# Infini-attention block on one NeuronCore: value products in three f16 parts

## The chip, the cores and the metric

The kernel runs on one NeuronCore of a Trainium2 chip. The metric is the device time of one execution in microseconds (us). Engines are named as in the profile: PE is TensorE (matmuls and its transposes), DVE VectorE, ACT ScalarE, POOL GpSimd, SP SyncE, which here only issues DMAs. Each engine works through its own list of instructions in order and waits at semaphores for the others.

## The reference

One block of two halves over x of shape (8, 512, 256) in f32: normalised attention with a compressive memory, then a coupled feed-forward part of three cycles. The change is in the attention. Its core, for segments of 128 rows and 16 heads of width 64:

```python
def step(carry, seg):
    M, Z = carry
    ...
    scores = jnp.einsum('bhid,bhjd->bhij', q, k) * scale
    scores = jnp.where(mask, -jnp.inf, scores)
    att_dot = jnp.einsum('bhij,bhjv->bhiv', jax.nn.softmax(scores, axis=-1), v)
    sq = jax.nn.elu(q) + 1.0
    att_mem = jax.lax.stop_gradient(sq @ M / (sq @ jnp.swapaxes(Z, -2, -1)))
    sk = jax.nn.elu(k) + 1.0
    M_new = M + jnp.einsum('bhld,bhlv->bhdv', sk, v)
    Z_new = Z + sk.sum(axis=-2, keepdims=True)
    att = gate * att_mem + (1.0 - gate) * att_dot
    out = att.reshape(B, LSEG, H * DV) @ Wo
    return ((M_new, Z_new), out)
```

The product that changes is the one of the softmax numerators with v (att_dot). A column of ones beside v gives the row sums, so that the division comes after the product: 65 columns for each head.

## The kernel before

**Staging.** Eight batches are taken as four pairs (bp), each with four segments (s): 16 steps, m = 4 bp + s. In a step the 32 units (2 batches by 16 heads) go in four groups (g) of 8 units, and a group's read-out in two halves of 4 units. Every engine has a hand-written function `step(bp, s)` that lists its work in order; nothing is scheduled by a program. After the 16 steps comes the feed-forward part (from about 880 us), which the change leaves alone.

**One group, in the order of its dependences.** PE computes scores (`scores`, L1266 to L1278, three f16 products of high and low parts of q and k) into the two banks `s_bank`. DVE takes the negated row maxima (`maxima`, L941). ACT exponentiates into Pr (`probs`, L658, 8 instructions). PE turns Pr, four units at a time, back into `s_bank` (`turn_probs`, L1288), and ACT copies the turned probabilities to the tile PT in f32 (`take_p`, L665, two instructions), which releases `s_bank` and the read-out (semaphore p_done). PE's `read_out` multiplies PT with V (L1301), sq with the memory M (L1307) and, after the second half, sk with V for the update of M (L1315). DVE divides by the row sums and adds the update (`divide`, L948 to L959). POOL mixes the memory and the dot part (`gated`, L467 to L471, three instructions for each half), and when all eight halves of a step are in, DVE transposes the result (`to_rows`, L1007) for the output projection (L1328, L1343).

**Beside it** PE computes the q, k and v of the next step (`project`, L1237, six pieces i = 0 to 5, 12 f16 matmuls of 512 columns each); DVE moves each piece out by a transpose (`take_x`, L916; pieces 4 and 5 are V) and so frees the banks `x_bank` for the next piece. `turn` (L1253) turns q and k of a group; ACT and DVE split them in high and low parts (`take_q`, L925 and L926; `take_k`, L934), and `scores` waits for both. ACT and POOL form elu(k) + 1 (`exp_k`, L647 and L651; `elu_k`, L452 and L454), not where s is 3.

**Orders that the prediction uses.** On PE a step is: scores(0), read_out(3,1) of the step before, project(0), turn_probs and turn of group 1, project(1), read_out(0,0), scores(1), turn_att, read_out(0,1), project(2), turn_att, turn_probs, project_out, turn, read_out(1,0), turn, project(3), scores(2), read_out(1,1), turn_probs and turn of group 3, project(4), read_out(2,0), scores(3), read_out(2,1), turn_probs and turn of the next group 0, read_out(3,0), project(5). In front of scores(1) DVE does take_x(5), maxima(0), divide(3,1), take_x(0), to_rows, take_q(1), take_k(1). to_rows waits until POOL has done gated(3,0) and gated(3,1) of the step before; POOL does them between elu_k(0) and elu_k(1). In front of scores(3) DVE ends with x2_norm (L876), take_q(3), take_k(3); at the end of a step it does take_x(4), take_q(0), take_k(0), divide(3,0), take_x(5), of which project(5) waits for take_x(4).

## Time and profile before

| | us |
|---|---|
| median of 3 runs | 1073.15 |
| lowest, highest | 1071.67, 1073.36 |
| the profiled execution | 1072.58 |
| its span, first to last instruction | 1070.8 |
| PE busy (matmul records) | 992.2, 93% |
| PEld busy (weight loads) | 698.9, 65% |
| DVE busy | 777.6, 73% |
| ACT busy | 635.1, 59% |
| POOL busy | 575.9, 54% |
| all L1301 matmul records (the f32 value products) | 136.0, 1024 records |

A matmul record lasts from its start to a modelled end, so records overlap; what one costs in a row of them is the distance between starts. An f32 matmul leaves two records, an f16 one leaves one. In brackets a timeline row has the idle time in front of it and what released it. The granted clock is 0.5 at 1.2 GHz and 1.0 at 2.4 GHz.

### The profile page before, as it was taken

The page shows a single profiled execution, that of the slowest core. Times are in us where ns is not written, and L with a number is a line of the kernel's source. Part 1 is how long each engine was busy: PE and PEld are TensorE (multiplying, and loading weights), DVE is VectorE, ACT ScalarE, POOL GpSimd, SP SyncE. Part 2 cuts the span into 40 slices and gives each one's busy share as a digit, 9 for nine tenths or more (in the row PEclk, how much of TensorE's full clock was granted, in tenths as well). Part 3 has the DMA queues.
Part 4 walks back from the last instruction along what each step waited for, and adds up shares of the span by engine and source line. Part 5 has one row for each costly group of instructions (what it writes and reads, how often), then busy time and mean ns, then how long its engine had stood idle before and what let it go on. Part 6 is the DMA issues. An engine that isn't in the chain of part 4 may idle for free.

```text
span 1070.8 us, 20177 instructions
## 1 busy us (share of the span) xinstructions
PE 992.2 (93%) x7748; PEld 698.9 (65%) x7748; DVE 777.6 (73%) x1399; ACT 635.1 (59%) x1364; POOL 575.9 (54%) x686
## 2 busy tenths in 40 slices
PE   5999999999999999999999999999999889999971
PEld 2677777776777777777777777777777765343431
DVE  6868687867777777768686868586959463588665
ACT  4756565556656564657474646474746454687863
POOL 4456565445656563456565635475747261456563
PEclk9999999999999999999999999999999989999995
DMA  7100000000000000000000000000000000300015
GB/s 187 32 21 1 21 2 21 2 21 1 21 2 21 2 21 1 21 1 21 1 21 2 21 2 21 1 21 1 12 2 16 18 11 10 157 1 1 1 40 118
DMA packets 16910, 23.92 MB, mean 22 GB/s; under 512 B 7344, under 2 KB 9136, under 8 KB 16304
## 3 DMA queue, kind: packets, MB, share of 16 engines
q1 hardware_dynamic: 15344, 18.58, 6.3%
q10 hardware_dynamic: 1472, 4.06, 1.1%
q8 instruction: 62, 1.02, 0.4%
q14 instruction: 32, 0.26, 0.1%
HBM read 13.97 MB, written 8.65 MB: 21 GB/s over the span
## 4 chain that ended last, share of the span: by engine, by line
PE 70%; DVE 19%; ACT 4%; POOL 3%; issue 3%; POOLq 0%; DVEq 0%; ACTq 0%
PE ps L1237 18%; PE ps L1343 11%; PE ps L1301 6%; PE ps L1278 5%; DVE arena L916 4%; PE ps L1470 4%; PE ps L1307 3%; PE ps L1483 3%; PE ps L1288 3%; PE ps L1328 3%; PE ps L1465 3%; PE ps L1253 3%; DVE arena L876 2%; PE ps L1315 2%; DVE arena L941 2%
## 5 line engine op out<-in xcount | busy, mean ns | idle before, releaser
L1237 PE MATMUL ps<-arena 128*128 128x512 f16 x1152 | 266.0, 381 | 5.2 <-DVE arena L893 3.1
L658 ACT ACTIVATE arena<-ps,arena 128x128 f32<-128x128 f32 x512 | 139.4, 387 | 96.1 <-DVE arena L941 96.1
L1237 PEld LDWEIGHTS ps<-arena 128*128 128x128 f16 x1152 | 110.2, 98 | 125.6 <-DVE arena L916 4.5
L916 DVE STREAM_TRANSPOSE arena<-ps 128x1024 f32<-128x1024 f32 x96 | 145.6, 1516 | 23.7 <-PE ps L1237 21.6
L467 POOL TENSOR_TENSOR arena<-arena 128x256 f32<-128x256 f32 x128 | 93.1, 728 | 125.0 <-DVE arena L951 82.0
L1301 PE MATMUL ps<-arena 128*128 128x65 f32 x1024 | 136.0, 276 | 5.9 <-ACT arena L665 4.8
L1301 PEld LDWEIGHTS ps<-arena 128*128 128x128 f32 x1024 | 127.5, 192 | 18.8 <-ACT arena L665 8.3
L868 DVE BATCH_NORM_STATS2 arena<-arena 128x6 f32<-128x256 f32 x100 | 36.9, 409 | 121.8 <-ACT arena L684 121.0
L1343 PE MATMUL ps<-arena 128*128 128x256 f32 x544 | 121.9, 382 | 0.3 <-ACT arena L672 0.3
L452 POOL TENSOR_TENSOR arena<-arena 128x512 f32<-128x512 f32 x48 | 73.2, 1526 | 86.9 <-ACT arena L651 86.6
L1343 PEld LDWEIGHTS ps<-arena 128*128 128x128 f32 x544 | 102.0, 190 | 16.1 <-ACT arena L672 1.4
L471 POOL TENSOR_TENSOR arena<-arena 128x256 f32<-128x256 f32 x128 | 95.2, 744 | 10.0
L420 POOL TENSOR_TENSOR arena<-arena 128x2 f32<-128x2 f32 x50 | 9.8, 195 | 167.6 <-DVE arena L872 167.6
L469 POOL TENSOR_TENSOR arena<-arena 128x256 f32<-128x256 f32 x128 | 93.4, 730 | 10.0
L665 ACT ACTIVATE arena<-ps 128x512 f32<-128x512 f32 x128 | 76.7, 615 | 33.6 <-PE ps L1288 33.6
L951 DVE TENSOR_TENSOR arena<-ps,arena 128x512 f32<-128x512 f32 x128 | 88.5, 691 | 4.4
L941 DVE TENSOR_REDUCE arena<-ps 128x4 f32<-128x512 f32 x128 | 80.8, 671 | 12.6 <-PE ps L1278 12.6
L1307 PE MATMUL ps<-arena 128*128 128x130 f32 x512 | 85.7, 289 | 0.0
L672 ACT ACTIVATE arena<-ps 128x512 f32<-128x512 f32 x68 | 37.2, 597 | 76.1 <-PE ps L1328 76.1
L1288 PE MATMUL ps<-arena 128*128 128x128 f32 x512 | 77.7, 279 | 4.4 <-ACT arena L658 4.3
L1253 PE MATMUL ps<-arena 128*128 128x128 f32 x512 | 77.3, 273 | 0.0
L876 DVE TENSOR_SCALAR arena<-arena 128x256 f32<-128x256 f32 x100 | 62.5, 665 | 18.4 <-POOL arena L422 18.0
(120 smaller groups left out, 1786.6 us busy)
## 6 DMA issues: line engine op xcount, KB each, us to landing
x_rows<-arena SPq DMA_DIRECT2D x17, 256.0 KB, 2.0
arena<-x_rows SPq DMA_DIRECT2D x4, 1024.0 KB, 7.9
arena<-in_L_attn_x_dram SPq DMA_DIRECT2D x124, 32.0 KB, 1.7
out_dram<-arena SPq DMA_DIRECT2D x26, 128.0 KB, 2.9
arena<-in_L_attn_Wq_dram ACTq DMA_DIRECT2D x2, 512.0 KB, 4.8
arena<-in_L_attn_Wk_dram ACTq DMA_DIRECT2D x2, 512.0 KB, 6.4
arena<-in_L_attn_Wv_dram ACTq DMA_DIRECT2D x2, 512.0 KB, 7.9
arena<-in_L_attn_Wo_dram SPq DMA_DIRECT2D x8, 128.0 KB, 4.7
```

Source lines behind the costliest of these rows:

```text
L467: pool.tensor_tensor(mem, mem, dot, ALU.subtract).then_inc(mix, 1)
L469: pool.tensor_tensor(mem, mem, gt, ALU.mult).then_inc(mix, 1)
L471: pool.tensor_tensor(att.rearrange("p (e y r h) -> p y h r e", y=2, r=2, h=HP)[:, g // 2, h:h + 2], mem, dot, ALU.add).then_inc(att_done, 1)
L658: last = act.activation(Pr[:, par, j, :], s_bank[:, par, j * P:(j + 1) * P], ACT.Exp, bias=negm[:, par, j:j + 1])
L916: dve.transpose(dst[:, d0:d0 + 32], bank.rearrange("p w (d c) -> p d w c", c=C)).then_inc(x_free, 1)
L941: dve.tensor_reduce(negm[:, par, :], s_bank[:, par, :].rearrange("p (j i) -> p j i", j=GP), AX.X, ALU.max, negate=True).then_inc(m_done, 1)
L1237: last = pe.matmul(bank[:, w, :], xc[:, lx, k, w * P:(w + 1) * P], W16[lw][:, k, i, :], start=(n == 0), stop=(n == 5))
L1253: last = pe.transpose(t_bank[b][:, j * P:(j + 1) * P], heads(src[par])[:, g // 2, GP * (g % 2) + j], identf)
L1288: last = pe.transpose(s_bank[:, par, j * P:(j + 1) * P], Pr[:, par, j, :], identf)
L1301: pe.matmul(pm_bank[:, 0, u * DV1:(u + 1) * DV1], PT[:, par, j, :], v[:, GP * (g % 2) + j, par, 0:DV1], start=True, stop=True)
L1307: last = pe.matmul(pm_bank[:, 1, a * 2 * DV1:(a + 1) * 2 * DV1], sqT[g % 2][:, j, :], M[:, GP * g + j, :, :], start=True, stop=True)
L1343: last = pe.matmul(t_bank[b][:, w * D:(w + 1) * D], attT[:, w, j, :], Wo_sb[:, j, :], start=(j == 0), stop=(j == 7))
```

## The change

The f32 tile PT becomes two f16 tiles of half the size, a high part (the f16 rounding) and a low part (what is left), and V gets the same pair, `vsplit`, for one step at a time. Each f32 value product (65 columns, two records) is replaced by three f16 products: high by high, high by low, low by high. Who makes the parts:

- ACT's `take_p` writes the high part of P instead of the f32 copy (same count of instructions); DVE gets `low_p`, two subtractions of 128x512 for each group, which now give p_done, and so release `read_out` and the next `scores`.
- ACT gets `v_high`, one copy of 128x520 for each group; POOL gets `v_low`, one subtraction of 128x520 for each group, and `read_out` waits for it.
- The tile attT (turned attention) takes the place of nat, its source, piece by piece; this adds no instruction and no wait, since each piece is copied out of PSUM only after the transposes of that piece have read it.
- ACT waits for the ones beside V (init 5) before its first take_q.

The update of the memory (sk with V) stays in f32.

```diff
--- before.py
+++ after.py
@@ -117,12 +117,15 @@
         xcur = [alloc(TILE, F16).rearrange("p (l k r) -> p l k r", l=2, k=KT) for _ in range(2)]
         sk = alloc(UNITS * DK)
         ek = alloc(GU * DK)
-        PT = alloc(GU * P).rearrange("p (h j i) -> p h j i", h=2, j=GP)
+        PT = [alloc(GU * P // 2, F16).rearrange("p (h j i) -> p h j i", h=2, j=GP) for _ in range(2)]
         Pr = alloc(GU * P).rearrange("p (h j i) -> p h j i", h=2, j=GP)
         AB = [alloc(2 * 4 * DK).rearrange("p (m u e) -> p m u e", m=2, u=4) for _ in range(2)]
         assert top[0] - late_off >= 2 * KT * PAIRS * NSEG * P
         nat = alloc(2 * H * DK).rearrange("p (w e c) -> p w e c", w=2, c=C)
-        attT = alloc(2 * H * DK).rearrange("p (w j r) -> p w j r", w=2, j=8)
+        attT = nat.rearrange("p w e c -> p (w e c)").rearrange("p (w j r) -> p w j r", w=2, j=8)
+        VE = DV1 + 1
+        vsplit = [alloc(UNITS * VE // 2, F16).rearrange("p (g r h e) -> p g r h e", g=GROUPS, r=2, h=GP)
+                  for _ in range(2)]
         identf = alloc(P)
         ident2 = alloc(P // 4, BF16)
         ones = alloc(P // 2, BF16)
@@ -227,7 +230,8 @@
         m_done = sem("m_done")
         e_done = sem("e_done")
         pt_full = sem("pt_full")
-        p_done = sem("p_done")
+        p_hi, p_done = sem("p_hi"), sem("p_done")
+        vh_done, vl_done = sem("vh_done"), sem("vl_done")
         rk_done = sem("rk_done")
         ek_done = sem("ek_done")
         sk_part = sem("sk_part")
@@ -306,6 +310,11 @@
         fn_done = sem("fn_done")
         o_done, od_done = sem("o_done"), sem("od_done")
 
+        def v_units(s, g):
+
+            return v_pos[s % 2].rearrange("p (y r h e) -> p y r h e", y=2, r=2, h=HP)[
+                :, g // 2, :, GP * (g % 2):GP * (g % 2) + GP, 0:DV1]
+
         def sk_count(bp, s, g):
 
             return bp * 4 * (NSEG - 1) + 4 * s + g
@@ -471,6 +480,12 @@
                     pool.tensor_tensor(att.rearrange("p (e y r h) -> p y h r e", y=2, r=2, h=HP)[:, g // 2, h:h + 2],
                                        mem, dot, ALU.add).then_inc(att_done, 1)
 
+                def v_low(bp, s, g):
+
+                    pool.wait_ge(vh_done, 4 * (bp * NSEG + s) + g + 1)
+                    hi, lo = (v[:, g, :, :, 0:DV1] for v in vsplit)
+                    pool.tensor_tensor(lo, v_units(s, g), hi, ALU.subtract).then_inc(vl_done, 1)
+
                 def y_dev(bp, s):
 
                     deviation(r_rs, r_mv, y_stat, y_rstd, bp * NSEG + (s + 1))
@@ -487,12 +502,16 @@
                 def step(bp, s):
                     m = bp * NSEG + s
                     elu_k(bp, s, 0)
+                    v_low(bp, s, 0)
                     if m > 0:
                         gated(*before(bp, s), 3, 0)
                         gated(*before(bp, s), 3, 1)
                     elu_k(bp, s, 1)
+                    v_low(bp, s, 1)
                     gated(bp, s, 0, 0)
                     gated(bp, s, 0, 1)
+                    v_low(bp, s, 2)
+                    v_low(bp, s, 3)
                     if m < NT - 2:
                         deviation(n_rs, n_mv, n_stat, n_rstd, m + 3)
                     y_dev(bp, s)
@@ -662,9 +681,15 @@
                 def take_p(bp, s, g):
                     for par in range(2):
                         act.wait_ge(pt_full, bp * 32 + 8 * s + 2 * g + par + 1)
-                        last = act.activation(PT[:, par, :, :].rearrange("p j i -> p (j i)"), s_bank[:, par, :],
-                                              ACT.Copy)
-                    last.then_inc(p_done, 1)
+                        act.activation(PT[0][:, par, :, :].rearrange("p j i -> p (j i)"), s_bank[:, par, :],
+                                       ACT.Copy).then_inc(p_hi, 1)
+
+                def v_high(bp, s, g):
+                    m = bp * NSEG + s
+                    act.wait_ge(x_free, 6 * m + 6)
+                    if m > 0:
+                        act.wait_ge(pm_full, 8 * (m - 1) + 2 * g + 2)
+                    act.activation(vsplit[0][:, g, :, :, 0:DV1], v_units(s, g), ACT.Copy).then_inc(vh_done, 1)
 
                 def take_a(job, i):
                     b, n = job
@@ -692,12 +717,16 @@
                 def step(bp, s):
                     ahead, last = bp * NSEG + s < NT - 2, bp * NSEG + s == NT - 1
                     exp_k(bp, s, 0)
+                    v_high(bp, s, 0)
+                    v_high(bp, s, 1)
                     probs(bp, s, 0)
                     take_p(bp, s, 0)
                     if s == 0 and bp > 0:
                         reset(*before(bp, s), 3)
                     take_q(bp, s, 1)
                     exp_k(bp, s, 1)
+                    v_high(bp, s, 2)
+                    v_high(bp, s, 3)
                     take_a(t_job(bp, s, "A0"), 0)
                     take_a(t_job(bp, s, "A1"), 1)
                     probs(bp, s, 1)
@@ -725,6 +754,7 @@
                     reset(bp, s, 2)
 
                 act.sem_inc(p_done, 1)
+                act.wait_ge(init, 5)
 
                 take_q(0, -1, 0)
                 act.wait_ge(m_in, 64)
@@ -941,6 +971,14 @@
                         dve.tensor_reduce(negm[:, par, :], s_bank[:, par, :].rearrange("p (j i) -> p j i", j=GP),
                                           AX.X, ALU.max, negate=True).then_inc(m_done, 1)
 
+                def low_p(bp, s, g):
+                    G = bp * 16 + 4 * s + g
+                    for par in range(2):
+                        hi, lo = (t[:, par, :, :].rearrange("p j i -> p (j i)") for t in PT)
+                        dve.wait_ge(p_hi, 2 * G + par + 1)
+                        last = dve.tensor_tensor(lo, s_bank[:, par, :], hi, ALU.subtract)
+                    last.then_inc(p_done, 1)
+
                 def divide(bp, s, g, half):
                     n = 8 * s + 2 * g + half
                     rd = pm_bank[:, :, 0:4 * DV1].rearrange("p m (u e) -> p m u e", u=4)
@@ -1017,6 +1055,7 @@
                     if not last:
                         take_x(bp, s, 0)
                     to_rows(bp * 32 + 8 * s + 8)
+                    low_p(bp, s, 0)
                     take_q(bp, s, 1)
                     take_k(bp, s, 1)
                     divide(bp, s, 0, 0)
@@ -1030,6 +1069,7 @@
                         take_x(bp, s, 2)
                     if ahead:
                         n_norm((s + 2) % 4, m + 3)
+                    low_p(bp, s, 1)
                     y_stats(bp, s)
                     take_q(bp, s, 2)
                     divide(bp, s, 1, 0)
@@ -1043,6 +1083,7 @@
                     x2_stats(bp, s)
                     divide(bp, s, 1, 1)
                     x2_norm(bp, s)
+                    low_p(bp, s, 2)
                     take_q(bp, s, 3)
                     take_k(bp, s, 3)
                     divide(bp, s, 2, 0)
@@ -1051,6 +1092,8 @@
                     divide(bp, s, 2, 1)
                     if not last:
                         take_x(bp, s, 4)
+                    low_p(bp, s, 3)
+                    if not last:
                         take_q(bp, s, 0)
                         take_k(bp, s, 0)
                     divide(bp, s, 3, 0)
@@ -1293,13 +1336,13 @@
                     n = 8 * s + 2 * g + half
                     v = v_pos[s % 2].rearrange("p (y r h e) -> p y h r e", y=2, r=2, h=HP)[:, g // 2]
                     pe.wait_ge(p_done, bp * 16 + 4 * s + g + 2)
-                    if g == 0:
-                        pe.wait_ge(x_free, bp * 24 + 6 * s + 6)
+                    pe.wait_ge(vl_done, 4 * (bp * NSEG + s) + g + 1)
                     pe.wait_ge(pm_free, bp * 32 + n + 1)
                     for u in range(4):
                         j, par = 2 * half + u // 2, u % 2
-                        pe.matmul(pm_bank[:, 0, u * DV1:(u + 1) * DV1], PT[:, par, j, :],
-                                  v[:, GP * (g % 2) + j, par, 0:DV1], start=True, stop=True)
+                        for i, (lp, lv) in enumerate(((0, 0), (0, 1), (1, 0))):
+                            pe.matmul(pm_bank[:, 0, u * DV1:(u + 1) * DV1], PT[lp][:, par, j, :],
+                                      vsplit[lv][:, g, par, j, 0:DV1], start=(i == 0), stop=(i == 2))
                     if s == 0:
                         pe.wait_ge(m_reset, bp * 8 + 2 * (g + 1))
                     for a in range(2):
```

**DVE, end of one step and start of the next.** The rows run from divide(2,1) (L948 to L959; L986 to L997 after) over take_x(4) (32x32 transposes), take_q(0), take_k(0). Before:

```order
L948 RECIPROCAL arena<-ps 128x8
L951 TENSOR_TENSOR arena<-ps,arena 128x512
L959 TENSOR_TENSOR arena<-ps,arena 64x4x65 x2
L916 STREAM_TRANSPOSE arena<-ps 128x32x32
L925 SCALAR_TENSOR_TENSOR arena<-ps,arena 128x512
L926 SCALAR_TENSOR_TENSOR arena<-ps,arena 128x512
L934 SCALAR_TENSOR_TENSOR arena<-ps,arena 128x512
```

After:

```order
L986 RECIPROCAL arena<-ps 128x8
L989 TENSOR_TENSOR arena<-ps,arena 128x512
L997 TENSOR_TENSOR arena<-ps,arena 64x4x65 x2
L946 STREAM_TRANSPOSE arena<-ps 128x32x32
L979 TENSOR_TENSOR arena<-ps,arena 128x512 x2
L955 SCALAR_TENSOR_TENSOR arena<-ps,arena 128x512
L956 SCALAR_TENSOR_TENSOR arena<-ps,arena 128x512
L964 SCALAR_TENSOR_TENSOR arena<-ps,arena 128x512
```

The two subtractions of low_p(3) (L979) stand between take_x(4) and take_q(0). In front of take_q(3) there is the same pair behind x2_norm (L906), and in front of take_q(1) behind to_rows, as the next piece shows.

**DVE, in front of scores(1):** take_x(0), to_rows (two transposes), take_q(1), take_k(1). Before:

```order
L916 STREAM_TRANSPOSE arena<-ps 128x32x4x8
L1007 STREAM_TRANSPOSE arena<-arena 128x32x2x16 x2
L925 SCALAR_TENSOR_TENSOR arena<-ps,arena 128x512
L926 SCALAR_TENSOR_TENSOR arena<-ps,arena 128x512
L934 SCALAR_TENSOR_TENSOR arena<-ps,arena 128x512
```

After:

```order
L946 STREAM_TRANSPOSE arena<-ps 128x32x4x8
L1045 STREAM_TRANSPOSE arena<-arena 128x32x2x16 x2
L979 TENSOR_TENSOR arena<-ps,arena 128x512 x2
L955 SCALAR_TENSOR_TENSOR arena<-ps,arena 128x512
L956 SCALAR_TENSOR_TENSOR arena<-ps,arena 128x512
L964 SCALAR_TENSOR_TENSOR arena<-ps,arena 128x512
```

Here low_p(0) stands between to_rows and the splits of q and k of group 1.

**POOL, start of a step:** elu_k(0) (L452, L454; L461, L463 after), then gated(3,0) and gated(3,1) of the step before, then elu_k(1). Before:

```order
L452 TENSOR_TENSOR arena<-arena 128x512
L454 TENSOR_TENSOR arena<-arena 128x512
L467 TENSOR_TENSOR arena<-arena 128x256
L469 TENSOR_TENSOR arena<-arena 128x256
L471 TENSOR_TENSOR arena<-arena 128x2x2x64
L467 TENSOR_TENSOR arena<-arena 128x256
L469 TENSOR_TENSOR arena<-arena 128x256
L471 TENSOR_TENSOR arena<-arena 128x2x2x64
L452 TENSOR_TENSOR arena<-arena 128x512
L454 TENSOR_TENSOR arena<-arena 128x512
```

After:

```order
L461 TENSOR_TENSOR arena<-arena 128x512
L463 TENSOR_TENSOR arena<-arena 128x512
L487 TENSOR_TENSOR arena<-arena 128x8x65
L476 TENSOR_TENSOR arena<-arena 128x256
L478 TENSOR_TENSOR arena<-arena 128x256
L480 TENSOR_TENSOR arena<-arena 128x2x2x64
L476 TENSOR_TENSOR arena<-arena 128x256
L478 TENSOR_TENSOR arena<-arena 128x256
L480 TENSOR_TENSOR arena<-arena 128x2x2x64
L461 TENSOR_TENSOR arena<-arena 128x512
L463 TENSOR_TENSOR arena<-arena 128x512
L487 TENSOR_TENSOR arena<-arena 128x8x65
```

v_low(0) (L487) now stands in front of the two gated, and v_low(1) behind elu_k(1).

## Rows read from the trace of the kernel before

**Rows 1.** The page: span, and busy time of each engine (share of the span), instructions.

```profile
span 1070.8 us, 20177 instructions
...
PE 992.2 (93%) x7748; PEld 698.9 (65%) x7748; DVE 777.6 (73%) x1399; ACT 635.1 (59%) x1364; POOL 575.9 (54%) x686
```

**Rows 2.** Timeline, PE, step m = 9 (s = 1): start us, us, engine, line.

```profile
508.87 0.40 PE L1266 MATMUL ps<-arena 64*64 64x512 bf16 x2
...
509.20 0.84 PE L1278 MATMUL ps<-arena 64*128 64x128 f16 x24
509.98 1.10 PE L1301 MATMUL ps<-arena 128*128 128x65 f32 x8
...
519.07 1.00 PE L1301 MATMUL ps<-arena 128*128 128x65 f32 x8
519.91 0.67 PE L1307 MATMUL ps<-arena 128*128 128x130 f32 x4
520.69 0.40 PE L1266 MATMUL ps<-arena 64*64 64x512 bf16 x2
...
541.51 0.40 PE L1266 MATMUL ps<-arena 64*64 64x512 bf16 x2
...
552.07 0.40 PE L1266 MATMUL ps<-arena 64*64 64x512 bf16 x2
...
557.59 1.11 PE L1301 MATMUL ps<-arena 128*128 128x65 f32 x8 [0.24 <-ACT arena L665]
...
559.31 2.76 PE L1237 MATMUL ps<-arena 128*128 128x512 f16 x12
562.01 0.40 PE L1266 MATMUL ps<-arena 64*64 64x512 bf16 x2
```

**Rows 3.** Timeline, DVE, the same step.

```profile
508.98 2.06 DVE L916 STREAM_TRANSPOSE arena<-ps 128x1024 f32<-128x1024 f32 x1
...
516.45 2.37 DVE L1007 STREAM_TRANSPOSE arena<-arena 128x1024 f32<-128x1024 f32 x2 [0.26 <-POOL arena L471]
518.74 0.65 DVE L925 SCALAR_TENSOR_TENSOR arena<-ps,arena 128x512 f32<-128x512 f32 x1
...
551.28 0.68 DVE L934 SCALAR_TENSOR_TENSOR arena<-ps,arena 128x512 f16<-128x512 f32 x1
...
557.19 2.07 DVE L916 STREAM_TRANSPOSE arena<-ps 128x1024 f32<-128x1024 f32 x1
```

**Rows 4.** Timeline, POOL, the same step: gated(3,1) of the step before.

```profile
514.03 0.72 POOL L467 TENSOR_TENSOR arena<-arena 128x256 f32<-128x256 f32 x1 [0.57 <-DVE arena L959]
```

**Rows 5.** Timeline, ACT, the same step: the second half of take_p(3).

```profile
556.94 0.60 ACT L665 ACTIVATE arena<-ps 128x512 f32<-128x512 f32 x1 [0.26 <-PE ps L1288]
```

**Rows 6.** Timeline, DVE, take_q(0) of a step with s = 3 (m = 7).

```profile
452.67 0.69 DVE L925 SCALAR_TENSOR_TENSOR arena<-ps,arena 128x512 f32<-128x512 f32 x1 [0.97 <-ACT arena L630]
```

**Rows 7.** Groups by line and form: busy us, mean ns of one, idle before.

```profile
L893 DVE TENSOR_TENSOR arena<-ps,arena 128x512 f16<-128x512 f32 x16 | 10.9, 680 | 0.2 <-ACT arena L598 0.2
L529 POOL TENSOR_TENSOR arena<-arena 128x512 f16<-128x512 f32 x16 | 22.6, 1429 | 1.6 <-ACT arena L785 1.6
```

**Rows 8.** Groups by line and form, weight loads of f16 and of f32.

```profile
L1237 PEld LDWEIGHTS ps<-arena 128*128 128x128 f16 x1152 | 110.2, 98 | 125.6 <-DVE arena L916 4.5 <-DVE arena L893 3.5 <-issue 2.5
L1301 PEld LDWEIGHTS ps<-arena 128*128 128x128 f32 x1024 | 127.5, 192 | 18.8 <-ACT arena L665 8.3 <-issue 1.3
```

**Rows 9.** Timeline, PE, four places where PE had waited.

```profile
467.53 0.40 PE L1266 MATMUL ps<-arena 64*64 64x512 bf16 x2 [1.36 <-DVE arena L926]
...
678.92 0.40 PE L1266 MATMUL ps<-arena 64*64 64x512 bf16 x2 [1.38 <-DVE arena L926]
...
839.94 0.64 PE L1266 MATMUL ps<-arena 64*64 64x512 bf16 x2 [4.09 <-DVE arena L926]
...
1023.33 0.63 PE L1446 MATMUL ps<-arena 128*128 128x128 f32 x4 [2.69 <-ACT arena L797]
```

**Rows 10.** Window behind the second of these: window, length, busy (x) of each engine, PEclk, DMA.

```profile
679.50:682.90 3.40, 3.40 (x34) 3.20 (x29) 2.49 (x4) 0.95 (x2) 3.24 (x4) 0.51 0.03 5
```

## The prediction, made before the changed kernel had run

> **What bounds the kernel now.** I read the page first: PE is busy for 93% of the span, the other three for 54% to 73% [rows 1]. Taken alone that invites the reading that any PE time saved is time saved. So I took one step of the attention apart in the timelines of PE, DVE, POOL and ACT, to see what stands directly in front of each `scores`, because the four groups follow one another through it. In step m = 9, scores(0) to scores(3) and the next scores(0) start at 508.87, 520.69, 541.51, 552.07 and 562.01 [rows 2]. That makes four stretches of 11.82, 20.82, 10.56 and 9.94 us, 53.14 in all. Three of them end on DVE's own list, though PE has next to no gaps:
> - In front of scores(1) DVE runs to_rows, take_q(1) and take_k(1) without a gap. to_rows had waited for POOL's gated, and started at 516.45; the three splits start at 518.74 and scores(1) comes 1.95 later [rows 2, 3].
> - In front of scores(3) take_k(3) runs from 551.28 to 551.96, and scores(3) starts at 552.07 [rows 2, 3].
> - At the end of the step take_x(4) ends at 557.19 + 2.07 = 559.26. project(5) needs the bank that this frees and starts at 559.31 [rows 2, 3].
>
> The second stretch is PE's, at least up to the end of project_out. PE and DVE are thus bound in turn, and DVE has no slack at the three places above.
>
> **The change, part by part.** Times in a stretch count from its first scores.
>
> *The product on PE.* The 8 records of a half's value product take 519.91 - 519.07 = 0.84 us before [rows 2]. Afterwards there are 12 f16 products of 65 columns, each with a load of 128 weight columns. No row has that form. The nearest is L1278: 24 f16 products of 128 columns, loads included, from 509.20 to 509.98, which is 0.78 / 24 = 32.5 ns each [rows 2]; 12 of them give 0.39 us, a saving of 0.45. The other end is the spacing of the f32 records, 0.84 / 8 = 105 ns: 1.26 us, a loss of 0.42. I take 0.45, since a f16 load lasts 98 ns where a f32 load lasts 192 [rows 8] and L1278 starts its loads at least as often as the new product must. The Trainium skill (TensorE: Matmul & The Clock Gate, "LDWEIGHTS (loading the stationary operand)") prices a load by its columns alone, at columns / 1.2 ns, whatever the type. By that, 12 loads would be 1.28 us and the product dearer than before; the spacing of 32.5 ns at L1278 speaks against it. All 128 halves at 0.45 would be 57.6 us, if PE were the bound everywhere.
>
> *low_p on DVE.* It is the operation of L893 (f16 out, PSUM minus an f16 tile, 128x512): 0.68 us [rows 7]. In a row such operations start 0.6 apart, so the two of a group take 1.2 on DVE's list; 64 groups make 77 us of DVE work. What counts is where they stand.
> - Third stretch: low_p(2) stands in front of take_q(3) and take_k(3), and scores(3) waits for them. +1.2; PE's savings there vanish in the wait. 11.76.
> - Fourth stretch: low_p(3) stands behind take_x(4) and has its high part long before (ACT's copy ends at 557.54, [rows 5]). take_x(4) ends at 7.19, low_p(3) at about 8.45. read_out(3,0), which before started at 557.59, that is at 5.52 [rows 2], now starts there. It takes 0.39 for the value product and about 0.55 for L1307, and only then comes project(5), which took 562.01 - 559.31 = 2.70 [rows 2]: 8.45 + 0.95 + 2.70 = 12.1 against 9.94. +2.15. Before, read_out(3,0) was hidden under take_x(4); now it comes after it.
> - Second stretch: low_p(1) falls in the time in which DVE waits for the output projection, and costs nothing. PE saves one product, read_out(0,1): -0.45. What read_out(1,0) saves is lost, since scores(2) again waits for splits that start from the end of project_out.
>
> *v_high and v_low in front of gated.* First stretch. take_x(5) ends at 508.98 + 2.06 = 511.04, at 2.17 [rows 3]; only then is V whole. ACT's copy of it costs about 0.6, as L665 for 512 elements [rows 5], and ends at 2.85. POOL's subtraction costs about 1.43, by L529 with its f16 output [rows 7], and ends at 4.3. It stands in front of both gated. A gated takes from 514.03 to the start of to_rows at 516.45, so 2.4 [rows 3, 4]; the pair ends at 9.1, where before it ended at 7.55, since the second had only to wait for divide(3,1), until 5.16. Then follow to_rows with 518.74 - 516.45 = 2.3, low_p(0) with 1.2 and the splits with 1.95: 9.1 + 2.3 + 1.2 + 1.95 = 14.55 against 11.82. +2.75, of which 1.55 is POOL's and 1.2 DVE's. The second v_high delays probs(0) by some 0.6, which the wait hides; v_low(1), (2) and (3) fall in front of uses that are 7 us and more away. L467's 0.72 for 256 elements [rows 4] would make 1.46 of v_low's 520, so its price is narrow; 0.3 either way is 5 us over the kernel. The far ends are no delay at all, should POOL start it early, and 1.55 + 0.6 should it wait for both copies: 25 us less, or 9 more.
>
> *At no cost:* attT over nat, the wait for init 5, take_p with f16 output.
>
> *Sum of a step:* 2.75 - 0.45 + 1.2 + 2.15 = +5.65. Over 14 steps 79. In the three of them with s = 3 DVE has 0.97 idle behind take_x(4) [rows 6], and the last stretch loses about 0.5 less: -1.5. The first step has no gated in front of to_rows and the last has no projections, so I count half for each: 5.6. Together 83 us. The profiled execution had 1072.6 us, so 1155.7 so far.
>
> *The clock.* PE now waits in every step for 2.9 us in front of read_out(0,0) (project(1) ends at 10.2 less the 0.45 saved before it, low_p(0) at 12.6) and for some 3.2 us in front of read_out(3,0) (turn ended at 5.52 - 0.24 [rows 2], low_p(3) ends at 8.45), and for a shorter time in front of read_out(2,0). In the trace PE was slow directly behind a wait of 4.09 and one of 2.69: the first L1266 record there lasts 0.64 where it lasts 0.40 elsewhere [rows 2, 9]. Behind a wait of 1.38 the clock fell to 1.2 GHz too, and stayed there for 3.4 us [rows 9, 10]; behind one of 1.36 at the same place of another step it did not (L1266 at 0.40, [rows 9]). Half speed for 3.4 us takes at most 1.7 us of work; a part of it lies in waits, so I take 1.4. With 15 steps, two long waits in each and two in three of them followed by a fall, that is 20 falls or 28 us. The Trainium skill (TensorE: Matmul & The Clock Gate, "HAM oscillation — how this bites in real kernels") describes just this for a loop that waits in every turn: the array goes back to half rate each time. By that all 30 would fall, 42 us.
>
> 1155.7 + 28 = 1183.7; the median of the runs lies 0.6 over the profiled execution. **Forecast 1184 us.**
>
> **Rivals.**
> - *No falls of the clock.* The waits are broken by a short read-out, and the wait of 1.36 left the clock alone; against it stand the waits of 2.69 and 4.09. 1156 us, or down to 1140 if DVE's chain is a little shorter than I add up.
> - *The clock falls at nearly every wait, or the f16 product is bound by its loads.* 45 waits at 1.6 make 72 us: 1228. A product of 1.26 us costs 0.87 more at two places in 16 steps, 28 us: 1212. The wait of 2.69 speaks for the first, L1278 against the second.
> - *Faster: PE is the bound, and the added work fits in idle time.* The page's 93% against 73% speaks for it. Its place is low_p(2) and low_p(3): they would have to end before PE gets to scores(3) and project(5). The point from which it decides is a slack of 1.2 us for DVE at these two places. The trace has 0.1 and 0.05 [rows 2, 3]. If it held, all 128 savings would count: 1073.2 - 57.6 = 1016 us.
> - *In between:* the chains are half as long as I say, because something that I take as serial overlaps: about 1110.
>
> **How the numbers follow.** Forecast with some falls (1165 to 1200) 0.5; no falls (1135 to 1165) 0.2; many falls or slow loads (1200 to 1235) 0.2; in between (1080 to 1135) 0.06; hidden, faster, 0.03; within 0.2%, 0.01. A measurement can tell this kernel from itself to about 0.2%. Leaving one in ten at either side, the range is 1136 to 1222. Faster 0.03, same 0.01, slower 0.96.
>
> **What would show it.** In the profile after: value products at about 0.4 us a half, against 0.84; DVE busy near 855 and POOL near 665; a step of 58 to 61 us. In the timeline scores(1) some 14.5 us behind scores(0), with read_out(0,0) released by DVE's low_p; to_rows released by POOL's gated at about 9.1; project(5) some 9.4 behind scores(3). Stretches of 3.4 us with a granted clock of 0.5 behind the long waits. The prediction is wrong if to_rows is no later than before (v_low not on the path), if read_out(2,0) and (3,0) don't wait for DVE, or if the clock stays at 1.0 in the attention; the last alone takes 28 us away.

## The result, and the profile after

The changed kernel takes 1192 us in the median of eight runs (1188.7 to 1195.1) where the kernel before takes 1072.8. In the first comparison the ratio was 1.1106 with a 95% interval of 1.1082 to 1.1131, in a second one 1.1118 (1.1103 to 1.1133). It is 11% slower, by 119 us; forecast were 1184 us, range 1136 to 1222.

Two further executions of the first comparison took 1228.3 and 1228.7 us and are left out of it; a trace of one of them has the same 14.1 us in the first stretch of a step, and a mean granted clock of 0.893 instead of 0.927. The profile below is of an execution of the same kernel that took 1189.4 us. It comes from the second comparison, for which this stood on record:

> The changed kernel itself, timed again beside the others. The theory: the same chains every time, about 1150 us of them, and above that what the falls of the clock add, which depends on where in a step the falls begin; so single runs between 1185 and 1230 us, the stretches without a fall at 14.1, 20.3, 11.8 and 12.0 us. The rival (a run-to-run difference of another kind): stretches that differ where the granted clock is 1.0.

A fall is a time in which the granted clock is 0.5 instead of 1.0. The stretches without a fall came out as written there, 14.1, 20.3 and 11.8 us. The fourth has a fall in every step with s below 3 and takes 13.3 to 14.5 us there; where s is 3 it takes 10.9 or 12.6. The runs of this comparison all lay between 1189.4 and 1195.1.

The page, for [rows 1]; busy time (share of the span) and instructions:

```profile
span 1187.6 us, 21518 instructions
...
PE 993.5 (84%) x8260; PEld 665.5 (56%) x8260; DVE 851.9 (72%) x1527; ACT 666.4 (56%) x1428; POOL 645.7 (54%) x750
```

PE's busy time is about what it was, though the value products got shorter, because a part of the work now runs at half the clock. DVE has 74 us more, ACT 31, POOL 70. No engine is more than 84% busy: the kernel got slower by waiting, and by what the waits do to the clock.

The timeline of PE in a step with s = 1 (m = 9), for [rows 2]; scores are L1309 here, the value product is L1344, the piece project(5) L1280, turn_rows L1255:

```profile
575.90 0.40 PE L1309 MATMUL ps<-arena 64*64 64x512 bf16 x2
...
577.01 0.54 PE L1344 MATMUL ps<-arena 128*128 128x65 f16 x12
577.39 0.69 PE L1350 MATMUL ps<-arena 128*128 128x130 f32 x4
...
588.19 0.84 PE L1344 MATMUL ps<-arena 128*128 128x65 f16 x12 [2.47 <-DVE arena L979]
588.84 1.22 PE L1350 MATMUL ps<-arena 128*128 128x130 f32 x4
590.03 0.63 PE L1309 MATMUL ps<-arena 64*64 64x512 bf16 x2
...
610.91 0.40 PE L1309 MATMUL ps<-arena 64*64 64x512 bf16 x2 [0.33 <-issue]
...
620.83 0.54 PE L1344 MATMUL ps<-arena 128*128 128x65 f16 x12 [2.05 <-DVE arena L979]
...
622.12 1.09 PE L1255 MATMUL ps<-arena 128*128 128x128 f32 x4 [0.22 <-DVE arena L956]
623.13 0.64 PE L1309 MATMUL ps<-arena 64*64 64x512 bf16 x2
...
632.14 0.76 PE L1344 MATMUL ps<-arena 128*128 128x65 f16 x12 [2.88 <-DVE arena L979]
632.72 1.22 PE L1350 MATMUL ps<-arena 128*128 128x130 f32 x4
633.73 3.73 PE L1280 MATMUL ps<-arena 128*128 128x512 f16 x12
637.38 0.40 PE L1309 MATMUL ps<-arena 64*64 64x512 bf16 x2
```

Three things are to be seen. First, the product itself: 577.39 - 577.01 = 0.38 us for 12 products, 32 ns each, against 0.84 for the 8 f32 records before. Second, three waits of 2.47, 2.05 and 2.88 us in front of a value product, all released by DVE's low_p (L979); before there was one of 0.24. Third, what comes behind the waits is slow: L1309 lasts 0.63 or 0.64 instead of 0.40, L1350 1.22 instead of 0.69, and project(5) 3.73 instead of 2.75.

The timelines of DVE and POOL in the first stretch of that step, for [rows 3, 4]. L487 is v_low, L476 to L480 one gated, L1045 to_rows, L979 low_p:

```profile
576.01 2.03 DVE L946 STREAM_TRANSPOSE arena<-ps 128x1024 f32<-128x1024 f32 x1 [2.63 <-PE ps L1280]
...
584.59 2.37 DVE L1045 STREAM_TRANSPOSE arena<-arena 128x1024 f32<-128x1024 f32 x2 [1.92 <-POOL arena L480]
586.89 1.25 DVE L979 TENSOR_TENSOR arena<-ps,arena 128x512 f16<-128x512 f32 x2
588.06 0.68 DVE L955 SCALAR_TENSOR_TENSOR arena<-ps,arena 128x512 f32<-128x512 f32 x1
```

```profile
578.79 1.14 POOL L487 TENSOR_TENSOR arena<-arena 128x520 f16<-128x520 f32 x1 [4.27 <-ACT arena L692]
579.88 0.73 POOL L476 TENSOR_TENSOR arena<-arena 128x256 f32<-128x256 f32 x1
...
583.81 0.74 POOL L480 TENSOR_TENSOR arena<-arena 128x256 f32<-128x256 f32 x1
```

The chain reads: take_x(5) to 578.04, v_high and v_low to 579.93, two gated to 584.55, to_rows, low_p(0), splits, scores(1) at 590.03. to_rows had waited 0.26 us for POOL before and waits 1.92 now.

And the granted clock (the column before the last two) over the whole step, over 6.4 us around the last wait, and in the three falls of the step, one behind each wait:

```profile
575.90:637.38 61.48, 52.97 (x497) 38.06 (x496) 45.71 (x83) 33.99 (x75) 36.84 (x43) 0.92 0.04 10
```

```profile
631.00:637.40 6.40, 5.25 (x32) 2.88 (x32) 3.78 (x7) 2.23 (x4) 2.92 (x3) 0.73 0.00 0
```

```profile
587.90:591.30 3.40, 3.11 (x34) 2.44 (x36) 3.20 (x7) 0.30 (x1) 3.32 (x4) 0.50 0.00 0
622.00:625.40 3.40, 3.28 (x38) 2.36 (x39) 1.57 (x4) 0.60 (x1) 2.89 (x4) 0.50 0.25 52
632.30:635.70 3.40, 3.40 (x21) 2.12 (x19) 2.48 (x5) 0.93 (x2) 2.28 (x2) 0.50 0.00 0
```

The step takes 61.48 us instead of 53.14.

### The profile page after: what moved, and what is told of

The parts are those of the page before. It is cut to its first block, busy times and chain, and to the rows that moved or that the text cites. A ratio compares the mean times of both kernels' runs of the same rounds, so it can differ in the third digit from the quotient of the medians.

```text
span 1226.9 us, 21518 instructions
## 1 busy us (share of the span) xinstructions
PE 1026.1 (84%) x8260; PEld 688.4 (56%) x8260; DVE 852.8 (70%) x1527; ACT 667.2 (54%) x1428; POOL 644.4 (53%) x750
## 3 DMA queue, kind: packets, MB, share of 16 engines
q8 instruction: 66, 1.08, 0.4%
## 4 chain that ended last, share of the span: by engine, by line
PE 55%; DVE 28%; POOL 8%; issue 4%; ACT 3%; POOLq 0%; DVEq 0%
PE ps L1280 13%; PE ps L1386 10%; DVE arena L946 6%; DVE arena L979 5%; PE ps L1350 5%; PE ps L1321 4%; PE ps L1371 4%; PE ps L1344 3%; PE ps L1513 3%; PE ps L1526 3%; DVE arena L1045 3%; DVE arena L971 3%; DVE arena L906 3%; PE ps L1508 2%; POOL arena L480 2%
## 5 line engine op out<-in xcount | busy, mean ns | idle before, releaser
L1280 PE MATMUL ps<-arena 128*128 128x512 f16 x1152 | 292.6, 409 | 3.8 <-DVE arena L923 3.0
L1280 PEld LDWEIGHTS ps<-arena 128*128 128x128 f16 x1152 | 118.8, 105 | 142.5 <-issue 36.0
L476 POOL TENSOR_TENSOR arena<-arena 128x256 f32<-128x256 f32 x128 | 92.9, 726 | 173.6 <-DVE arena L989 88.2
L1344 PE MATMUL ps<-arena 128*128 128x65 f16 x1536 | 78.9, 207 | 117.5 <-DVE arena L979 116.4
L1344 PEld LDWEIGHTS ps<-arena 128*128 128x128 f16 x1536 | 65.7, 106 | 141.7 <-DVE arena L979 134.1
L487 POOL TENSOR_TENSOR arena<-arena 128x520 f16<-128x520 f32 x64 | 71.9, 1136 | 87.4 <-ACT arena L692 87.4
L461 POOL TENSOR_TENSOR arena<-arena 128x512 f32<-128x512 f32 x48 | 73.1, 1523 | 73.0 <-ACT arena L670 72.4
L1386 PEld LDWEIGHTS ps<-arena 128*128 128x128 f32 x544 | 102.0, 190 | 16.1 <-ACT arena L697 1.4
L1350 PE MATMUL ps<-arena 128*128 128x130 f32 x512 | 110.5, 349 | 0.0
L697 ACT ACTIVATE arena<-ps 128x512 f32<-128x512 f32 x68 | 38.5, 598 | 125.5 <-PE ps L1371 125.5
L480 POOL TENSOR_TENSOR arena<-arena 128x256 f32<-128x256 f32 x128 | 94.5, 739 | 10.0
L906 DVE TENSOR_SCALAR arena<-arena 128x256 f32<-128x256 f32 x100 | 62.4, 664 | 49.1 <-POOL arena L431 48.7
L692 ACT ACTIVATE arena<-arena 128x520 f16<-128x520 f32 x64 | 37.2, 629 | 108.0 <-DVE arena L946 99.2
L1331 PE MATMUL ps<-arena 128*128 128x128 f32 x512 | 78.3, 280 | 19.1 <-ACT arena L677 19.1
L684 ACT ACTIVATE arena<-ps 128x512 f16<-128x512 f32 x128 | 76.6, 615 | 19.1 <-PE ps L1331 19.0
L1350 PEld LDWEIGHTS ps<-arena 128*128 128x128 f32 x512 | 85.4, 236 | 0.0
```

Source lines behind the costliest of these rows:

```text
L476: pool.tensor_tensor(mem, mem, dot, ALU.subtract).then_inc(mix, 1)
L480: pool.tensor_tensor(att.rearrange("p (e y r h) -> p y h r e", y=2, r=2, h=HP)[:, g // 2, h:h + 2], mem, dot, ALU.add).then_inc(att_done, 1)
L906: last = dve.tensor_scalar(dst[:, w * D:(w + 1) * D], src[:, w * D:(w + 1) * D], mv[:, w, 0:1], rs[:, w:w + 1], ALU.subtract, ALU.mult)
L1280: last = pe.matmul(bank[:, w, :], xc[:, lx, k, w * P:(w + 1) * P], W16[lw][:, k, i, :], start=(n == 0), stop=(n == 5))
L1344: pe.matmul(pm_bank[:, 0, u * DV1:(u + 1) * DV1], PT[lp][:, par, j, :], vsplit[lv][:, g, par, j, 0:DV1], start=(i == 0), stop=(i == 2))
L1350: last = pe.matmul(pm_bank[:, 1, a * 2 * DV1:(a + 1) * 2 * DV1], sqT[g % 2][:, j, :], M[:, GP * g + j, :, :], start=True, stop=True)
```

## The experiments

All of them are read by the same four stretches, from one scores to the next, in the step m = 9. For orientation, the table first; the columns are us. One step doesn't stand for all where there are falls: the 21.92 in two of the rows below holds a fall, and 20.3 us is the length of that stretch without one.

| kernel | time | 1st | 2nd | 3rd | 4th |
|---|---|---|---|---|---|
| before | 1072.8 | 11.82 | 20.82 | 10.56 | 9.94 |
| the change | 1192 | 14.13 | 20.88 | 12.22 | 14.25 |
| the sum in the prediction, without the clock | 1156 | 14.55 | 20.37 | 11.76 | 12.1 |
| change, waits filled | 1150.8 | 14.11 | 20.32 | 11.75 | 11.82 |
| change, last wait filled | 1168.6 | 14.12 | 21.04 | 12.14 | 12.76 |
| change, v_low(0) behind gated | 1158.8 | 12.72 | 21.92 | 11.75 | 13.15 |
| change, pairs early too | 1125.6 | 12.75 | 21.92 | 11.26 | 12.62 |
| before + DVE pairs | 1182.9 | 13.05 | 20.82 | 11.88 | 15.66 |
| before + DVE pairs, waits filled | 1148.0 | 13.05 | 20.83 | 11.88 | 12.73 |
| before + V parts | 1095.5 | 12.94 | 20.82 | 10.57 | 9.95 |
| products alone | 1062.9 | 11.57 | 20.33 | 10.56 | 9.60 |
| P rounded once | 1059.2 | 11.55 | 20.21 | 10.55 | 9.58 |

The fences show the central lines of each edit. The theory was that of the prediction: the added work stands in the lists of DVE and POOL that release the next scores, and the waits that it gives PE bring the clock down. The rivals were that the product itself is dear, that PE is the bound, and that the loss comes from a single cause.

### The products alone

```diff
-                    low_p(bp, s, 0)
...
+                for t in (PT[1], vsplit[0], vsplit[1]):
+                    pool.memset(t, 0.5).then_inc(vl_done, 1)
```

With low_p(bp, s, 0) go all other calls of low_p, v_low and v_high; ACT's take_p releases the read-out, as before.

> The three f16 products of each value product, and none of the work that makes the parts: no subtraction on DVE, none on POOL, no copy of V on ACT. The low parts and both parts of V are constants that are filled in once, so the output is not the reference's. The theory (DVE's and POOL's chains set the pace at three places of a step): PE saves 0.47 us for each half, but only the one in the second stretch counts, and about 0.25 in the fourth, since take_x(4) comes that much sooner; 16 x 0.7 = 11 us, so 1061 us. The rival (PE is the bound, so that each of the 128 savings counts): 1072 - 60 = 1012 us. If the new products were themselves dear, the time would be above 1072.

Measured: 1062.9 us, ratio 0.9917 (0.9885 to 0.9948). 10 us are gained; filling in the constants delays the first scores by 4.5 us (39.0 us after the start instead of 34.5), so that the steps gain some 14. 128 shorter products at 0.46 would be 59. The second stretch gives 0.49, the fourth 0.34, the first 0.25, the third nothing. So the product is cheap, and PE's time is not the kernel's time: three quarters of what PE saves goes into waits. This bears out the central reading of the prediction.

### DVE's pairs alone

```diff
+                def low_p(bp, s, g):
+                    G = bp * 16 + 4 * s + g
+                    for par in range(2):
+                        dve.wait_ge(p_hi, 2 * G + par + 1)
+                        last = dve.tensor_tensor(scrap[:, par, :], s_bank[:, par, :],
+                                                 PT[:, par, :, :].rearrange("p j i -> p (j i)"), ALU.subtract)
+                    last.then_inc(p_done, 1)
```

> The kernel before with its f32 value products, plus one pair of 128x512 subtractions on DVE for each group, at the four places where the change has them, its result unused; the release of the read-out and of the next scores comes from DVE as in the change. The theory: +1.2 us in the first stretch, 0 in the second, +1.2 in the third, +2.6 in the fourth (the f32 read-out of 1.4 us now comes behind the pair), 5.0 for a step, about 75 us in all, and some 10 to 25 us for falls of the clock behind the wait of 3 us in the fourth: 1157 to 1172 us. The rival (the added DVE work fits in DVE's idle time, and POOL's subtraction and the clock make the loss): under 1090 us.

Measured: 1182.9 us, 11 above the upper end of what was expected. The first three stretches are as expected (+1.23, 0, +1.32); the fourth takes 15.66 instead of 12.54. The timeline of PE shows where the 3 us are (L1314 is the f32 value product, L1320 the memory product, L1250 project(5)):

```profile
624.92 1.97 PE L1314 MATMUL ps<-arena 128*128 128x65 f32 x8 [3.24 <-DVE arena L948]
626.69 1.18 PE L1320 MATMUL ps<-arena 128*128 128x130 f32 x4
627.66 4.47 PE L1250 MATMUL ps<-arena 128*128 128x512 f16 x12
632.06 0.40 PE L1279 MATMUL ps<-arena 64*64 64x512 bf16 x2
```

```profile
624.90:632.00 7.10, 7.08 (x24) 4.21 (x24) 2.66 (x5) 0.75 (x2) 4.96 (x5) 0.56 0.00 0
```

Behind a wait of 3.24 us the value product takes 1.77 instead of 0.94 and project(5) 4.4 instead of 2.7, at a granted clock of 0.56 over 7.1 us. The releaser, L948, is the pair in this kernel. The expectation had the fall too cheap: not 10 to 25 us but 35.

The same kernel with PE kept busy in its waits:

```diff
+                    pe.wait_ge(pm_free, bp * 32 + n + 1)
+                    if bp * NSEG + s < NT - 1 and half == 0:
+                        for _ in range((10, 0, 30, 48 if s < NSEG - 1 else 30)[g]):
+                            pe.matmul(pm_bank[:, 0, 6 * DV1:512], W16[0][:, 0, 0, 0:P],
+                                      W16[0][:, 0, 0, 0:512 - 6 * DV1], start=True, stop=True)
```

> The kernel before with f32 products and DVE's pairs (as in the run with the pairs alone, 1183 us), plus idle work for PE in its waits: 10, 30 and 48 (30 where s is 3) products of 122 columns in front of read_out(0,0), (2,0) and (3,0). The theory: the clock stays up, the fourth stretch takes 12.6 instead of 15.6 us, so 1183 less 11 x 3.0 = 1150 us; that is what the pairs cost by their place in DVE's list, and it is the same as for the whole change with filled waits. The rival (the 15.6 us have another cause than the clock): 1180 us.

Measured: 1148.0 us, 35 less with 1266 more products on PE. The fourth stretch is 12.73. So the pairs cost 75 us by their place in DVE's list, which is about their whole work on DVE (853.2 - 777.6 = 76 us), and the clock another 35. That the two agree is partly chance: the second pair of a step is hidden, and the fourth costs twice, since read_out(3,0) now comes behind take_x(4).

### The parts of V alone

```diff
+                    v_low(bp, s, 0)
                     if m > 0:
                         gated(*before(bp, s), 3, 0)
```

> The kernel before with its f32 products, plus ACT's copies and POOL's subtractions for V at their places in the change, results unused. The theory: v_low(0) releases to_rows 1.2 us later, so the first stretch takes 13.05 instead of 11.83 us, the other three stay; 15 x 1.2 = 18 us, perhaps 0.5 to 1.5 us more in some steps for a fall of the clock behind the longer wait: 1091 to 1105 us. The rival (POOL and ACT have the time, 54% and 59% busy): 1072 us.

Measured: 1095.5 us, ratio 1.0195 (1.0175 to 1.0215). The first stretch is 12.94, +1.12, and nothing else moved. 23 us, of which 15 x 1.1 = 17 are the chain, the rest steps with a longer second stretch: three of them, with 22.4 to 24.0 us instead of 20.8, where the kernel before has one. POOL and ACT have 40% of idle time in this kernel; it does not help work that stands in front of what others wait for. The V parts here have two waits more than in the change (ACT's copy and DVE's take_x of V wait for the subtractions of the step before), so that no tile is rewritten too early; no stretch shows them.

### v_low(0) behind the two gated

```diff
-                    v_low(bp, s, 0)
                     if m > 0:
                         gated(*before(bp, s), 3, 0)
                         gated(*before(bp, s), 3, 1)
+                    v_low(bp, s, 0)
```

> The changed kernel with POOL's first subtraction of a step moved behind the two gated that it stood in front of. The theory: to_rows is released 1.14 to 1.4 us sooner, read_out(0,0) still waits for DVE, so the first stretch is 12.8 instead of 14.1 us; 15 x 1.2 = 18 us less, and a shorter wait in front of read_out(0,0) brings fewer falls of the clock: 1160 to 1175 us against some 1190 for the changed kernel. The rival (V's low part is not on the path, its wait is hidden by low_p): 1190 us, no difference.

Measured: 1158.8 us, 33 less than the change and 1 below the lower end of what was expected. The first stretch is 12.72. The chain gives 15 x 1.4 = 21, the rest is fewer falls. to_rows now waits 0.50 us for POOL instead of 1.92:

```profile
569.75 2.37 DVE L1045 STREAM_TRANSPOSE arena<-arena 128x1024 f32<-128x1024 f32 x2 [0.50 <-POOL arena L480]
```

One moved line takes back a quarter of the loss.

### The waits filled

```diff
+                    pe.wait_ge(pm_free, bp * 32 + n + 1)
+                    if bp * NSEG + s < NT - 1 and half == 0:
+                        for _ in range((38, 0, 28, 42 if s < NSEG - 1 else 28)[g]):
+                            pe.matmul(pm_bank[:, 0, 6 * DV1:512], W16[0][:, 0, 0, 0:P],
+                                      W16[0][:, 0, 0, 0:512 - 6 * DV1], start=True, stop=True)
```

> The changed kernel with idle work for PE in its three long waits of a step: 38, 28 and 42 (28 where s is 3) f16 products of 122 columns into a part of the bank that nothing reads, about 51 ns each, in front of read_out(0,0), (2,0) and (3,0). They end before DVE releases the read-out. The theory (the waits bring the clock down, and this is worth 30 us and more): the granted clock stays at 1.0 through the attention, the stretches are 14.1, 20.4, 11.8 and 12.1 us, and the time is 1072 + 15 x 5.2 = 1150 us. The rival (the clock has another cause, or its falls cost little, and the chains themselves are longer than I added up): 1185 us or more, with falls as before.

Measured: 1150.8 us, 41 less than the change. PE in the step m = 9, around two of the waits (L1341 is the idle work, L1349 the value product), and the clock over the step:

```profile
563.64 2.19 PE L1341 MATMUL ps<-arena 128*128 128x122 f16 x38
566.25 0.54 PE L1349 MATMUL ps<-arena 128*128 128x65 f16 x12 [0.42 <-DVE arena L979]
...
605.26 2.40 PE L1341 MATMUL ps<-arena 128*128 128x122 f16 x42
608.39 0.54 PE L1349 MATMUL ps<-arena 128*128 128x65 f16 x12 [0.72 <-DVE arena L979]
...
609.30 2.75 PE L1280 MATMUL ps<-arena 128*128 128x512 f16 x12
```

```profile
553.98:611.98 58.00, 54.28 (x605) 41.09 (x605) 45.58 (x83) 34.01 (x75) 36.55 (x44) 1.00 0.04 10
```

The granted clock is 1.00 over the step, against 0.92 without the idle work. The second and third stretch have the length of the sum; the first is 0.44 and the fourth 0.28 shorter than in it. The 38 idle products take 2.19 us, 57 ns each instead of the 51 expected, and still end before DVE's release. This separates the two parts of the loss: 78 us of chains and 41 us of clock. The split is a little rough, since the filled run loses some 6 us of its own. In its first step the idle work is longer than the wait (first stretch 12.70, in the change 11.21), its step m = 4 keeps one fall (second stretch 21.91), and in the last step, which has no idle work, the third stretch takes 14.03 us at a granted clock of 0.76, in the change 11.13. Without these, an estimate from the same rows, it is about 72 us of chains and 47 of clock.

With the last wait filled alone:

```diff
+                        for _ in range((0, 0, 0, 42 if s < NSEG - 1 else 28)[g]):
```

> The changed kernel with idle work for PE in front of read_out(3,0) alone: 42 products of 122 columns (28 where s is 3). The theory: no fall in the fourth stretch, which then takes 12.0 us; the wait of 2.5 to 2.9 us in front of read_out(0,0) still brings falls that cost 0.5 to 2.6 us in the second stretch. Of the 40 us between the changed kernel and the run with all three waits filled, the fourth stretch has about 12 x 2 = 24 and the others 16: 1165 us. The rival (one wait is enough to bring the clock down for the step): 1185 us or more.

Measured: 1168.6 us, 4 more than expected. Over the first 15 steps of the profiled runs, the fourth stretches together take 206.9 us in the change, 181.6 here and 176.1 with all waits filled: three quarters of what the falls cost lie there, not the three fifths that were expected. The fourth is not free of falls here either, 12.76 us in the step m = 9 at a granted clock of 0.90, since falls now begin behind the wait in front of read_out(2,0) and reach into it. And the second stretches together got longer, from 312.9 to 322.0 us (304.3 with all waits filled). So a fall that is prevented at one place partly comes back at another.

### The same work in another order on DVE

```diff
-                    x2_norm(bp, s)
                     low_p(bp, s, 2)
+                    x2_norm(bp, s)
...
+                    low_p(bp, s, 3)
                     if not last:
                         take_x(bp, s, 4)
-                    low_p(bp, s, 3)
```

> The changed kernel with v_low(0) behind the two gated, low_p(3) in front of take_x(4) and low_p(2) in front of x2_norm; the same work in another order on DVE. The theory: first stretch 12.75, third 11.75 (DVE's list is as long as before), fourth: low_p(3) runs from 5.5 to 6.75 us, take_x(4) to 8.9, project(5) to 11.6 instead of 12.0, and read_out(3,0) starts at 6.8 instead of 8.25, so that PE's wait in the fourth stretch falls apart in two short ones and brings no fall: 1159 us of the run with v_low behind, less 15 x 0.4 and less 12 falls of 1.5: about 1135 us. The rival (the order of the pairs is of no account, since DVE's sum is what counts, and the falls stay): 1153 to 1159 us.

Measured: 1125.6 us, 33 less than with v_low(0) moved alone and 9 less than expected. The third stretch is shorter than DVE's list was said to allow, 11.26 against 11.75: x2_norm takes less of DVE's list behind the pair. In the change (first two rows) it is 619.48 - 617.72 = 1.76 us from its start to the next instruction, here 584.72 - 583.44 = 1.28:

```profile
617.72 1.73 DVE L906 TENSOR_SCALAR arena<-arena 128x256 f32<-128x256 f32 x2
619.48 1.29 DVE L979 TENSOR_TENSOR arena<-ps,arena 128x512 f16<-128x512 f32 x2
```

```profile
582.24 1.29 DVE L979 TENSOR_TENSOR arena<-ps,arena 128x512 f16<-128x512 f32 x2
583.44 1.35 DVE L906 TENSOR_SCALAR arena<-arena 128x256 f32<-128x256 f32 x2
584.72 0.67 DVE L955 SCALAR_TENSOR_TENSOR arena<-ps,arena 128x512 f32<-128x512 f32 x1
```

The trace of the change has the same two instructions once more, at 601.64, where POOL has nothing to do; there they take 0.74 us. In both rows above POOL is at work on gated beside them. That this makes them slow was not tried.

The expectation for the fourth stretch failed in part: it said 11.6 us and no fall. Without a fall it takes 11.0 us, but only four of the 15 steps have none there; in the others, as in m = 9, it takes 12.1 to 12.7 us.

The order alone is worth 66 us of the 119. No further order was tried on the other 53.

### A version that is faster than both

P is rounded once to f16, so that DVE's pairs and the third product fall away; V keeps both parts.

```diff
-                        for i, (lp, lv) in enumerate(((0, 0), (0, 1), (1, 0))):
+                        for i, (lp, lv) in enumerate(((0, 0), (0, 1))):
```

> The changed kernel without DVE's pairs: P is rounded once to f16 and has no low part, so that the third product (low by high) is left out; V keeps both parts, and v_low(0) stands behind the two gated. What is left out is the part of the result that P's low part carries. The theory: nothing new stands in DVE's chains, so PE's savings of 0.6 us count at the places where PE is the bound: first stretch 11.6 to 12.3, second 20.2, third 10.55, fourth 9.6: 1056 to 1062 us, faster than the kernel before by 1%. The rival (V's work on POOL and ACT costs wherever it stands): 1072 us or more.

Measured: 1059.2 us, ratio 0.9878 (0.9859 to 0.9897): 1.2% faster than the kernel before. Its value product takes 0.24 us:

```profile
511.58 0.41 PE L1340 MATMUL ps<-arena 128*128 128x65 f16 x8
511.82 0.69 PE L1346 MATMUL ps<-arena 128*128 128x130 f32 x4
513.59 0.40 PE L1305 MATMUL ps<-arena 64*64 64x512 bf16 x2 [1.08 <-DVE arena L957]
```

The last row shows the limit: scores(1) waits 1.08 us for DVE's split, so most of what PE saves in front of it is lost (the first stretch is 11.55 us against 11.82 before). It carries less of P than the change does.

## Why the prediction was right

The direction, the size and the two causes came out; the sum without the clock was 1156 us and the run with filled waits shows 1150.8. How near the total came is partly luck, as the last of the steps says. By its steps:

- **The product on PE**: 0.39 us forecast from L1278's spacing, 0.38 measured. The Trainium skill's price of a load by its columns (TensorE: Matmul & The Clock Gate, "LDWEIGHTS (loading the stationary operand)") would have made it dearer than before: 107 ns for each load of 128 columns, where 12 products with their loads come 32 ns apart in this trace. The section names no type; that it holds whatever the type was the prediction's reading, and this f16 load does not bear it out.
- **Third stretch**: +1.2 forecast, 11.76; measured 11.75 at full clock.
- **Fourth stretch**: 12.1 forecast, 11.82 measured at full clock (12.0 in the steps where s is 0 or 2). I had left out that divide(2,1), which waits for PE, comes sooner by what PE saves: 3.0 us behind scores(3) with the waits filled, 3.4 before.
- **Second stretch**: 20.37 forecast, 20.32 at full clock.
- **First stretch**: 14.55 forecast, 14.11 measured. The mechanism was right, the term that was too big is v_low: 1.43 us by L529, 1.14 measured, which is 0.29 of the 0.44.
- **The sum of a step**: +5.65 forecast, 58.00 - 53.14 = 4.86 measured in the step m = 9 at full clock, 0.8 too much. Over 14 steps that is 11 us. The filled run hides half of it, since it has some 6 us of losses of its own: without them the chains give about 1145 and not 1156.
- **The clock**: this term was too small. I put down 20 falls at 1.4 us, 28 us; the filled run gives 41, or 47 without its own losses. What failed is the count. In the profiled run the granted clock is down 35 times in the first 15 steps: 11 times behind the wait in front of read_out(0,0), 10 times behind the one in front of read_out(2,0), and 14 times behind the one in front of read_out(3,0). I had nothing for the second of these. The price was about right: these steps are 42 to 45 us longer than in the filled run, so 1.2 to 1.3 us a fall. Two of the 35 last 6.8 us, the others 3.4. That one wait can cost more than the 1.7 us that the prediction set as the most is shown by the pairs alone: there the fourth stretch loses 2.9 us, with the clock at 0.56 for 7.1 us. The 30 falls that stand in the prediction beside the 20 are nearer, yet the loop in that section of the Trainium skill (TensorE: Matmul & The Clock Gate, "HAM oscillation — how this bites in real kernels") waits some 3 to 5 us in each turn, where the waits here are 2.0 to 2.9 us.
- **The total**: 11 us too much for the chains and some 19 too little for the clock have opposite signs, and so the forecast of 1184 lies closer to 1192 than its parts deserve.

Of the signs named beforehand, most came: DVE 852 against 855, read_out(0,0), (2,0) and (3,0) released by DVE, to_rows released by POOL at 584.59 - 575.90 = 8.7 instead of 9.1, scores(1) 14.1 behind scores(0) instead of 14.5. POOL's 646 are below the 665 (v_low again). A step of 61.5 us is above the 58 to 61, and project(5) comes 10.6 us behind scores(3) instead of 9.4; both are the clock, for with the waits filled they are 58.0 and 9.1.

**The rivals.** Faster by 57 us was refuted by the products alone: 10 to 14 us, not 59. Slow loads are out by the product's 0.38 us. No falls at all did not happen. Falls at nearly every wait is nearer to the truth than the forecast was: 35 falls at 45 waits, 2.7 to 3.1 us a step.

## What to carry to other kernels

Before work is moved from a full engine to emptier ones, look at what stands directly in front of the instruction that everybody waits for: 76 us of DVE work in DVE's idle 27% cost 75 us, since three of four pieces stood in the chain. Place added work behind what others wait for, and in front of the engine's own long waits; here the same instructions in a better order cost 53 us instead of 119. And when the matrix engine begins to wait for two or three us in every turn of a loop, count the slow time behind each wait in with the wait: here it was over a third of the loss. Count every place with such a wait, the shorter ones too: the wait of 2.05 us brought 10 falls in 15 steps, the one of 2.47 us 11.

## What the runs showed of the hardware that was not expected

- A fall of the clock can be prevented by idle work. 1578 products into an unused part of a bank made the change 41 us faster, and the granted clock of a step went from 0.92 to 1.00.
- Waits of 2.0 to 2.9 us bring the clock down at most of their places, 35 of 45 in the profiled run of the change, and a fall costs 1.2 to 1.3 us on average. Preventing the falls at one place brings more at another: with the last wait filled alone the fourth stretches get 25 us shorter and the second ones 9 us longer.
- The subtraction of an f16 tile from an f32 tile into f16 takes POOL 1.13 to 1.15 us for 128x520 in the attention, and 1.15 to 1.60 us, 1.43 in the mean, for 128x512 in the feed-forward part [rows 7]. The cause was not tried.
